# Probability round trip reordered: transpose at the same half's end, SP loads block e-1 before it stores block e, other transfers spread over eight slots

## What is computed

```python
def _L0_xattn_ref(features, latents, key_attention_mask, ...):
    x = layer_norm(features, ln_m_w, ln_m_b)
    lat = layer_norm(latents, ln_l_w, ln_l_b)
    q = (lat @ Wq)...            # 16 heads of 64
    kv_in = jnp.concatenate([x, lat], axis=1)      # 64 + 64 keys
    k = (kv_in @ Wk)...; v = (kv_in @ Wv)...
    sim = jnp.einsum('bhqd,bhfd->bhqf', q * scale, k)
    sim = jnp.where(full_mask[:, None, None, :] == 0, -jnp.inf, sim)
    alphas = jax.nn.softmax(sim, axis=-1)
    out = jnp.einsum('bhqf,bhfv->bhqv', alphas, v)
    return out... @ Wo

def _L0_ffn_ref(x, gate_w, w1, w3, w2, ws1, ws3, ws2):
    scores = jax.nn.sigmoid(xt @ gate_w)
    top_scores, top_idx = jax.lax.top_k(scores, K)  # 2 of 8 experts
    ...
    h = silu(xt @ w1[e]) * (xt @ w3[e]);  y = h @ w2[e]
    return shared + sum over the two experts of score * y

x = x + _L0_xattn_ref(ctx, _layernorm(x), mask, ...)
x = x + _L0_ffn_ref(_layernorm(x), ...)
```

## Time and profile before

| | |
|---|---|
| median of 3 runs | 1158.64 us (1152.14 to 1159.47) |
| the profiled execution | 1153.85 us |
| its span, first to last instruction | 1152.1 us |
| busy: PE, PEld, DVE, ACT, POOL | 94%, 82%, 80%, 69%, 53% |
| DMA: moved, mean rate | 176.81 MB, 153 GB/s |
| store of a block / one of its four loads, issue to landing | 2.4 us / 2.2 us (medians) |
| a gates load of 256 KB, issue to landing | 4.2 us (median) |

### The profile page before, as it was taken

How to read it: one execution, slowest core, us unless ns; L and a number is a source line. 1 busy time by engine, 2 the same in 40 slices (tenths; PEclk the granted TensorE clock), 3 DMA queues, 4 the chain that set the end, 5 groups by cost and what they waited for, 6 DMA issues and landing times.

```text
span 1152.1 us, 28179 instructions
## 1 busy us (share of the span) xinstructions
PE 1083.4 (94%) x7720; PEld 941.8 (82%) x7720; DVE 926.4 (80%) x4095; ACT 792.1 (69%) x2924; POOL 615.2 (53%) x717
## 2 busy tenths in 40 slices
PE   6899999999999999999999999999999999999976
PEld 6788887888888788888888888888888888888755
DVE  3878887888887788888888888778888788888756
ACT  4887777776777677777776677776777776777631
POOL 5555555555555455555555555555555555554421
PEclk9999999999999999999999999999999999999979
DMA  5455455555455555455555555555455555545531
GB/s 153 141 165 155 152 169 161 163 153 154 150 170 155 162 147 159 145 172 161 171 155 154 154 158 170 168 152 149 137 168 168 168 151 154 155 149 163 157 117 33
DMA packets 248717, 176.81 MB, mean 153 GB/s; under 512 B 29424, under 2 KB 215408, under 8 KB 248560
## 3 DMA queue, kind: packets, MB, share of 16 engines
q1 hardware_dynamic: 247376, 173.96, 50.8%
q10 hardware_dynamic: 1184, 1.05, 0.3%
HBM read 103.35 MB, written 71.56 MB: 152 GB/s over the span
## 4 chain that ended last, share of the span: by engine, by line
SPq 26%; PE 24%; DVE 21%; DMA 11%; issue 11%; ACT 5%; POOL 0%; DVEq 0%; POOLq 0%; ACTq 0%
SPq L335 13%; DMA pT<-probsT_dram 9%; SPq L363 6%; PE bank L860 5%; PE bank L873 4%; PE bank L815 4%; PE bank L817 3%; PE bank L816 3%; SPq L328 3%; DVE logits L671 3%; DVE probsT L686 3%; ACT probs L557 3%; SPq L369 3%; DVE h L704 2%; DVE g_eq L603 2%
## 5 line engine op out<-in xcount | busy, mean ns | idle before, releaser
L453 POOL TENSOR_TENSOR probs<-probs,rdenom 128x512 f32<-128x512 f32 x256 | 266.4, 1041 | 405.0 <-DVE rdenom L680 400.4
L557 ACT ACTIVATE probs<-logits,neg_max 128x128 f32<-128x128 f32 x1024 | 398.7, 396 | 0.9 <-DVE neg_max L671 0.9
L873 PEld LDWEIGHTS bank<-kvT,tT 128*128 128x128 f32 x2048 | 268.8, 192 | 120.3 <-issue 106.8
L860 PE MATMUL bank<-pT,kv_f 128*128 128x512 f32 x512 | 269.3, 607 | 44.2 <-DMA pT<-probsT_dram 43.9
L873 PE MATMUL bank<-kvT,tT 128*128 128x128 f32 x2048 | 270.7, 275 | 0.0
L716 DVE TENSOR_TENSOR cT_lo<-bank,cT_hi 128x512 fp32r<-128x512 f32 x256 | 175.2, 685 | 83.8 <-ACT cT_hi L527 83.7
L671 DVE CUSTOM_DVE_ANT_0 logits<-bank,mask_add 128x128 f32<-128x128 f32 x1024 | 232.6, 282 | 6.1 <-PE bank L873 5.9
L527 ACT CAST cT_hi<-bank 128x512 fp32r<-128x512 f32 x256 | 150.0, 586 | 113.1 <-PE bank L860 112.5
L557 ACT ACTIVATION_READ_ACCUMULATOR probs<-logits,neg_max 128x1 f32 x1024 | 197.6, 193 | 0.0
L512 ACT ACTIVATE h_tanh<-bank 128x256 f32<-128x256 f32 x160 | 61.6, 385 | 180.7 <-PE bank L817 178.3
L686 DVE STREAM_TRANSPOSE probsT<-probs 128x512 f32<-128x512 f32 x256 | 176.0, 688 | 0.7 <-issue 0.5
(11 more groups left out here) (102 smaller groups left out, 1996.4 us busy)
## 6 DMA issues: line engine op xcount, KB each, us to landing
probsT_dram<-probsT SPq DMA_DIRECT2D x256, 256.0 KB, 2.4
pT<-probsT_dram SPq DMA_DIRECT2D x1024, 64.0 KB, 2.2
gates<-gates_dram SPq DMA_DIRECT2D x62, 256.0 KB, 4.2
kv_raw<-in_ctx SPq DMA_DIRECT2D x32, 128.0 KB, 2.8
kv_raw<-in_x SPq DMA_DIRECT2D x32, 128.0 KB, 2.9
mask_raw<-in_mask_BxS_ik SPq DMA_DIRECT2D x32, 128.0 KB, 3.4
x_res<-in_x SPq DMA_DIRECT2D x32, 128.0 KB, 2.7
out<-out_sb SPq DMA_DIRECT2D x32, 128.0 KB, 3.0
```

The lines of the kernel that those rows point to most:

```text
L453: nc.gpsimd.tensor_tensor(by_pair, by_pair, rdenom[n][:, :].unsqueeze(2).unsqueeze(3).broadcast_to([P, PAIRS, P // QUAD, QUAD]), ALU.mult) ...
L557: nc.scalar.activation(probs[c % 4][:, :, r, :], logits[c % 2][:, r, :].rearrange("p (c k) -> p c k", k=QUAD), ACT.Exp, bias=neg_max[c % 2 ...
L860: nc.tensor.matmul(C_ps[c % 2][:, :], kv_f[g % 3][:, kl % 4, :], pT[c % 3][:, :], start=True, stop=True).then_inc(C_in_psum, 1)
L873: last = nc.tensor.matmul(S_ps[c % 2][:, P * r:P * (r + 1)], tT[:, kl % 4, hd:hd + 2, :], kvT[g % 2][:, kl % 4, :], start=True, stop=True)
```

## The change

Three things change. VectorE transposes block e at the end of half e, behind `cT_lo`, and no longer block e-1 in the middle of half e. SP's slot of half e first issues the loads of block e-1 and then the store of block e; before, it was the store of e-1 and then the loads of e-2. The other transfers move in front of the load and store of their slot and go to other slots: gates loads from half 6 to half 0 of the next frame, mask from 0 to 1, `x_res` from 1 to 2, outputs from 0 to 3, gates stores from four in half 5 to two each in halves 5 and 6, keys from half 0 to half 7 of the frame before.

```diff
-                    if has_half(e - 1):
-                        store_probs(e - 1)
-                    if has_half(e - 2):
-                        load_probs(e - 2)
-                    if k == 0 and has(j, p, -1, NG - 3):
-                        load_kv(j, p + 2)
+                    if k == 0 and has(j, p, 3, NG + 1):
+                        sp.wait_ge(gates_stored, 64 * (i - 2))
+                        after(sp, h_routed_done, NT * (i - 3))
+                        ... (the two gates loads)
+                    if k == 1 and has(j, p, -1, NG - 3):
                         load_mask(j, p + 2)
-                    if k == 0 and has(j, p, 4, NG + 2):
-                        store_out(i - 1)
-                    if k == 1 and has(j, p, 0, NG - 1):
+                    if k == 2 and has(j, p, 0, NG - 1):
...
+                    if k == 3 and has(j, p, 4, NG + 2):
+                        store_out(i - 1)
+                    if k in (5, 6) and has(j, p, 2, NG):
...
+                        for a in (0, 1) if k == 5 else (2, 3):
...
+                    if k == 7 and has(j, p, -2, NG - 4):
+                        load_kv(j, p + 3)
+                    if has_half(e - 1):
+                        load_probs(e - 1)
+                    if has_half(e - 0):
+                        store_probs(e - 0)
...
@@ vector, behind rdenom
-                    if has_half(e - 1):
-                        c = e - 1
-                        dve.wait_ge(probs_ready, c + 1)
...
@@ vector, behind cT_lo
+                    if has_half(e):
+                        c = e
+                        dve.wait_ge(probs_ready, c + 1)
+                        if c >= 2:
+                            dve.wait_ge(probsT_stored[(c - 2) % 3], 16 * ((c - 2) // 3 + 1))
+                        nc.vector.transpose(probsT[c % 2][:, :], ...).then_inc(probsT_ready, 1)
```

More of the change, by code:

```diff
@@ L342, in frame @@
                     e = HALVES * i + k
-                    if has_half(e - 1):
-                        store_probs(e - 1)
-                    if has_half(e - 2):
-                        load_probs(e - 2)
-                    if k == 0 and has(j, p, -1, NG - 3):
-                        load_kv(j, p + 2)
+                    if k == 0 and has(j, p, 3, NG + 1):
+                        sp.wait_ge(gates_stored, 64 * (i - 2))
+                        after(sp, h_routed_done, NT * (i - 3))
+                        for a in range(2):
+                            sp.dma_start(gates[FH * a:FH * (a + 1), :, :],
+                                         gates_dram.rearrange("(r a) t -> a r t", a=2)[a, :, :].partition_broadcast(FH)
+                                         ).then_inc(gates_loaded, 16)
+                    if k == 1 and has(j, p, -1, NG - 3):
                         load_mask(j, p + 2)
-                    if k == 0 and has(j, p, 4, NG + 2):
-                        store_out(i - 1)
-                    if k == 1 and has(j, p, 0, NG - 1):
+                    if k == 2 and has(j, p, 0, NG - 1):
                         after(sp, x1_step, 3 * (i - 2) + 1)
@@ L357, in frame @@
                                      ).then_inc(x_res_loaded[p], 16)
-                    if k == 5 and has(j, p, 2, NG):
+                    if k == 3 and has(j, p, 4, NG + 2):
+                        store_out(i - 1)
+                    if k in (5, 6) and has(j, p, 2, NG):
                         sp.wait_ge(gate_step, GATE_STEPS * (i - 1))
                         after(sp, gates_loaded, 32 * (i - 2))
-                        for a in range(P // QUAD):
+                        for a in (0, 1) if k == 5 else (2, 3):
                             sp.dma_start(gates_dram.rearrange("e (t a q) -> e t a q", t=TT, a=P // QUAD)[:, :, a, :],
                                          g_denseT[QUAD * a:QUAD * a + E, :, :]).then_inc(gates_stored, 16)
[L365 to L371, removed]
+                    if k == 7 and has(j, p, -2, NG - 4):
[4 more added lines that the diff above has]
+                        store_probs(e - 0)
                 if i == NG + 2:
@@ L718, in frame @@
                                                 ALU.subtract).then_inc(cT_lo_ready, 1)
+                    if has_half(e):
[3 more added lines that the diff above has]
+                            dve.wait_ge(probsT_stored[(c - 2) % 3], 16 * ((c - 2) // 3 + 1))
+                        nc.vector.transpose(probsT[c % 2][:, :], probs[c % 4][:, :, :, :].rearrange("p c r k -> p (c r k)")
+                                            ).then_inc(probsT_ready, 1)
                     if k in (3, 4) and i < LAST:
```

## The result

The changed kernel is slower: 1209.95 us (median of 4 runs, 1207.91 to 1210.94) against 1157.64 us (median of 4, 1152.14 to 1159.47), ratio 1.0458 with the interval 1.0419 to 1.0497. The prediction was 1140, with a range up to 1172, so the sign was wrong and the range too. The profiled execution took 1207.91 us, its span 1206.2 against 1152.1.

A forecast was written before the change was run, and what follows sets the result against it. TensorE was taken as the bound, with 1.61 us a frame of waits for `pT`. 1153.85 - 15.1 (VectorE's loop) + 5.3 (SP's round) - 4 (ends) = 1140.0 us; likeliest range 1130 to 1146, 8 in 10 from 1112 to 1172.

The forecast's parts named there:

- What bounds the kernel: Steady part before the change: TensorE's own work 32.80 us a frame, plus 1.61 us of waits for `pT`.
- VectorE's loop: Halves 7 to 1: the moved transposition delays the gate product by 1.07 us; frame 33.87, saving 15.1 us over 28 frames.
- SP's round: SP's store, landing, four loads in series: 4.10 us a slot, 34.2 a frame; loss 5.3 us after earliness.
- The third rival: SP's round becomes the bound above 4.30 us a slot and the kernel slower: 1168 to 1213 us; chance 0.22.
- The 4 us of earliness absorb 4: Loads come about 4 us earlier, absorbing 4 of the 9.3 us that SP's round costs over 28 frames.
- C ahead of `pT`: idle under 10 us: Sign in the profile after: TensorE's idle time ahead of C, waiting for `pT`, under 10 us in all.
- The ends: Last frames: C's waits of 1.88 and 3.09 us go, 4 us counted as gain; the first C left uncounted.
- Checks that I named: Frames longer than 34.4 us would show it wrong; SP's waits for landings were put above 300 us in sum.

The follow-up runs named there:

- spread_only: Kernel before with only the other transfers moved to the changed kernel's slots, ahead of store and loads; 1110.29 us, ratio 0.9615.
- swap: Changed kernel with SP's slot in the other order, store of block e first, then loads of block e-1; 1134.50 us, ratio 0.9829.
- dve_only: Kernel before with only VectorE's transposition moved to the end of half e, SP's list untouched; 1139.99 us, ratio 0.9874.
- sp_only: Changed kernel with VectorE's transposition back as before; SP loads block e-2, then stores e-1; other transfers still spread; 1207.78 us, ratio 1.0471.
- three_buffers: Changed kernel with three `probsT` buffers instead of two; 1203.01 us, ratio 1.0444.
- dose_spread: A fifth, tiny load per block added to the kernel before with only the other transfers spread; 1136.65 us (+26.4), ratio 0.9871.
- others_moved: Kernel before with only keys, mask, `x_res` and outputs moved (halves 7, 1, 2, 3, in front), gates left; 1209.62 us, ratio 1.0467.

## Why the prediction was wrong

**What bounds the kernel: right.** TensorE's own frame of 32.80 us and 1.61 us of waits for `pT` were confirmed by `spread_only` (32.91).

**How the miss adds up.** The prediction had the span 13.8 us shorter; it is 54.1 longer. Of these 67.9 us, 40.3 lie in 28 frames of 35.64 instead of 34.2, 18.6 in the stretch ahead of frame 2, 4 in the earliness and 5.0 in the end.

**VectorE's loop: right, in mechanism and size.** Mark to gate product was put at 10.58; it is 10.58 in a frame of after where SP is not late, and 10.60 in `swap` and in `dve_only`. The frame was put at 33.87; it is 33.75 in `swap`. The prediction forecast this as the first limit, and it would have been, had SP kept up.

**SP's round: right in mechanism, wrong in size.** This is the term of the sum that failed. I put a plain slot at 4.10 us, 1.0 more for the gates, 0.4 for the rest: 34.2 a frame. Measured are 35.76. The gates slot is 1.1 above the others (5.44 against 4.33), so that part was right; the plain slots, with what the other transfers cost in them, average 4.33 and not 4.15. The typical landing was near what I had read, 2.2 us against 2.1. But of 224 landings outside the gates slot 31 took 2.7 us or more, about 1.2 us too long. Spread over 224 slots that is 0.17 each, which is nearly all of the difference between 4.33 and 4.15. I had read the typical row (2.1) and the median over all stores (2.5) and chose close to the first, arguing that the long ones stand behind gates and keys. Some stand behind nothing. A serial loop pays the mean of its landings, never the typical one, and can't win a late one back. The third rival named the point of decision, 4.30 us a slot; the mean slot is 4.47. Its mechanism is what happened. It got a chance of 0.22 and was cut from the range at its dearer half, where the time came to lie.

The Trainium skill, page "DMA: Bandwidth & Descriptors", section "Anatomy of one DMA", gives by its formula an estimate of 2.6 us for this store. Its heading and its fit are for transfers that GpSimd issues, which the prediction left out; these are issued by SP. The rounds above show 2.2 us for most and 2.52 from store to first load on the mean, with the late ones and the gates slot in it. The typical landing is below the page's figure; the mean of the loop lies near it.

**"The 4 us of earliness absorb 4": wrong.** There never was any. Up to the mark of frame 2 the kernel lost 18.6 us: 3.7 up to C of e = 8, 6.7 from there to C of e = 16, 8.2 in the seven halves behind it. TensorE's timeline in the fill, before (C of e = 8 and e = 16):

```profile
53.38 0.70 PE L860 MATMUL bank<-pT,kv_f 128*128 128x512 f32 x1 [0.40 <-DMA pT<-probsT_dram]
...
80.59 0.59 PE L860 MATMUL bank<-pT,kv_f 128*128 128x512 f32 x1
```

And after:

```profile
57.10 0.70 PE L861 MATMUL bank<-pT,kv_f 128*128 128x512 f32 x1 [1.22 <-DMA pT<-probsT_dram]
...
91.02 0.70 PE L861 MATMUL bank<-pT,kv_f 128*128 128x512 f32 x1 [1.19 <-DMA pT<-probsT_dram]
```

The first frames have no experts, so their halves are short, 3.40 us each before. SP's round doesn't shrink with them: after, they take 4.24. Not all of the 18.6 is SP's order, though. In `swap`, without the serial round, the mark of frame 2 still comes 3.9 us later than before:

```profile
113.18 1.02 PE L861 MATMUL bank<-pT,kv_f 128*128 128x512 f32 x2
```

`dve_only` has it at 112.61 and `spread_only` at 109.01, so these 3 to 4 us come with the move on VectorE and 14.8 with the serial round. The sum began at frame 2 and took the stretch ahead of it as unchanged ("the first C of all waits too; I leave what may be won there uncounted").

**"C ahead of `pT`: idle under 10 us": wrong by little, and for a reason that matters.** It is 15.8, of which 10.5 before 128 us. I took it that SP's lateness would show there. It shows at the gate product, through the two `probsT` buffers. Of the 52.9 us there some 29 are the wait that the prediction had (1 us in each of 29 frames; `swap` has 30.4), and the other 24 are SP's lateness. The change lets VectorE write a block a half earlier, into a buffer whose store is as late as SP; that path stood in the section on the order of things and in no step of mine.

**The ends:** I counted a gain of 4 us; the tail lost 1.0. In `swap`, without the serial round, it gains 4.1, so the 4 us were there to be had.

**Checks that I named:** frames above 34.4 us (35.64) and a sum of SP's waits near 300 (288.6) came out as signs of the bound round. They were the right ones to look at.

**What stays open.** Why about one plain landing in seven is late. The trace offers a companion. Two stores of the timeline above, by the DMA view of the 2.1 us behind each: the late one of 615.61 (landing 3.3 us) and the prompt one of 611.54 (2.2). In the stretch of the late one there is a queue that the other lacks:

```profile
q8 instruction: 1, 0.02, 3.3%
```

It is one packet of 16 KB of the kind that the profile calls instruction. Of the 31 late stores outside the gates slot 20 had such a packet in their first 2.1 us; of the 193 prompt ones 7 had. The traces of the other serial kernels show the same: 17 of 32 against 3 of 192 in `sp_only`, 24 of 40 against 1 of 184 in `three_buffers`. The kernel before has as many of these packets, 62, but SP seldom waits for a landing there. This is a coincidence in the traces and not shown as a cause: no run changes the number of these packets, and a third or more of the late stores have none.

## What to carry to other kernels

Where one list both starts a transfer and waits for its landing, ask what it could issue in the meantime, and put that in front of the wait: here the store of the next block ahead of the loads of this one is worth 75 us of 1210. If such a loop must be serial, price its round with the mean landing of all its transfers, in the shortest stretch of the program as well as in the steady one, and count no earliness that the fill has already used. Slack that is a mean over the frame is not slack in each slot (`dose_spread`). Spread other transfers first and measure, and see which ones come to stand next to each other (`others_moved` loses 57 us by that); a move of work that was to hide their burst (VectorE's transposition here) may be worth less than nothing once they are spread.

## What the runs showed of the hardware

- SP's issuing takes 0.43 us (median) for a load of 64 KB in this form (1.74 for four in a quiet slot, 1.73 to 1.97 on the mean of a half in the kernel after), 0.34 to 0.38 for a store of 256 KB, 0.55 for one right behind key loads, 0.33 for a load of 1 KB, and 0.61 to 0.65 for a key load of 128 KB: the form and the neighbours count, hardly the bytes.
- A store with other large transfers around it on SP's queue lands late: 3.5 us from store to first load on the mean in the slot of the gates loads, with the mask right behind, against 2.3 in the quiet halves, and 4.66 in the case shown.
- A small transfer appended to a block's loads is not free in a kernel whose issuing list has slack on the mean: 26 us over 256 blocks in `dose_spread`.
- The granted clock was 0.76 in the 14 us behind a stretch with a wait of 3.5 us of TensorE, and 0.993 on the mean of `three_buffers`, where no wait of C is longer than 3.0 us and most are under 1. In `others_moved` two matmuls of C took 2.08 us at the lower level and 1.12 at the full one.
